# First channels loaded in quarters, first query products in four PSUM banks with their high terms first, bias row cast in one piece

## The reference

```python
q = x @ Wq.T + bq;  k = x @ Wk.T + bk;  v = x @ Wv.T + bv      # then split into 16 heads
q = softmax(q, axis=-1)          # over the 16 channels of a head
k = softmax(k, axis=-2)          # over the 1024 tokens
state = einsum('bhnd,bhne->bhde', k, v)
out = einsum('bhnd,bhde->bhne', q, state)        # heads joined again
out = layernorm(out) * ln_g + ln_b
x = layernorm(x + out @ Wo.T + bo)
h = layernorm(x) * ln1_g + ln1_b
h = layernorm(gelu(h @ ternary(w1).T + b1)) * ln2_g + ln2_b
x = layernorm(x + h @ ternary(w2).T + b2)
```

## Time and profile before

| | us |
|---|---|
| median of 3 runs (range) | 558.14 (557.33 to 558.61) |
| the profiled execution, its own time | 558.38 |
| its span in the profile | 556.4 |
| PE busy in the span | 533.2 (96%) |
| PEld, DVE, ACT, POOL busy | 490.5, 481.3, 481.7, 405.7 |
| first row of the queries' products on PE | 6.18 |
| first row of the keys' products of batch 0 | 13.66 |
| first row of `q_product(1, 0)` | 19.27 |

### The profile page before, as it was taken

The page is one execution under the profiler, slowest core; times in us unless marked ns, Lnnn a source line. Parts: engine busy times, 40 slices in busy tenths (PEclk is TensorE's granted clock), DMA queues, the critical chain, the costliest instruction groups (busy, mean ns, idle before and its releaser), DMA issues. The chain is left out here.

```text
span 556.4 us, 10878 instructions
## 1 busy us (share of the span) xinstructions
PE 533.2 (96%) x3533; PEld 490.5 (88%) x3533; DVE 481.3 (86%) x1230; ACT 481.7 (87%) x955; POOL 405.7 (73%) x420
## 2 busy tenths in 40 slices
PE   8999999999999999989899999999999999999991
PEld 7999999898999989779788998999999999999890
DVE  5878998989899898948687899999999999999895
ACT  5746798798979878778889999999999999999993
POOL 3965979877787977476558876876776776676693
PEclk9999999999999999999999999999999999999996
DMA  8530050411605030241111022222012222110012
GB/s 340 201 113 0 4 226 2 173 56 69 234 1 228 1 115 39 75 155 75 76 40 33 13 71 77 77 76 68 39 50 77 77 77 77 45 34 38 39 39 113
DMA packets 12679, 46.51 MB, mean 84 GB/s; under 512 B 1360, under 2 KB 3792, under 8 KB 10448
## 3 DMA queue, kind: packets, MB, share of 16 engines
q1 hardware_dynamic: 12336, 45.28, 22.6%
q10 hardware_dynamic: 288, 0.54, 0.3%
HBM read 29.01 MB, written 16.81 MB: 82 GB/s over the span
## 5 line engine op out<-in xcount | busy, mean ns | idle before, releaser
L1957 PE MATMUL qps_sps_aps_then_y<-ff_w_over_xc_lo,ff_a_lo_over_qw 128*128 128x258 f32 x512 | 126.7, 283 | 0.0
L1957 PE MATMUL qps_sps_aps_then_y<-ff_w_over_xc_lo,ff_a_hi_over_xc_lo 128*128 128x258 f32 x512 | 126.6, 283 | 0.0
L1308 DVE SCALAR_TENSOR_TENSOR ff_a_lo_over_qw<-ring,ff_rho,ff_a_hi_over_xc_lo 128x512 fp32r<-128x512 f32 x128 | 93.0, 745 | 15.5 <-ACT ff_a_hi_over_xc_lo L847 14.6
L1933 PE MATMUL ring<-ff_ht_hi_over_qw,t 128*128 128x512 f32 x256 | 104.0, 406 | 0.9 <-DVE ff_ht_lo_over_xc_hi L1300 0.5
L1933 PE MATMUL ring<-ff_ht_lo_over_xc_hi,t 128*128 128x512 f32 x256 | 100.7, 393 | 0.0
L1957 PEld LDWEIGHTS qps_sps_aps_then_y<-ff_w_over_xc_lo,ff_a_hi_over_xc_lo 128*128 128x128 f32 x512 | 96.9, 189 | 3.6
L1957 PEld LDWEIGHTS qps_sps_aps_then_y<-ff_w_over_xc_lo,ff_a_lo_over_qw 128*128 128x128 f32 x512 | 96.6, 189 | 3.4
L829 ACT ACTIVATE ring<-ring,bias 128x512 f32<-128x512 f32 x128 | 84.0, 685 | 7.8 <-PE ring L1933 6.8
L553 POOL TENSOR_TENSOR ff_accp_over_xt_lo<-ff_accp_over_xt_lo,ff_sq_over_ek_et_hi 128x512 f32<-128x512 f32 x66 | 86.1, 1304 | 2.9
L845 ACT ACTIVATE ff_sq_over_ek_et_hi<-ring 128x512 f32<-128x512 f32 x128 | 80.6, 630 | 0.5
L847 ACT CAST ff_a_hi_over_xc_lo<-ring 128x512 fp32r<-128x512 f32 x128 | 79.5, 621 | 0.0
(11 more groups left out here) (191 smaller groups left out, 1605.0 us busy)
## 6 DMA issues: line engine op xcount, KB each, us to landing
xt<-in_x_tok_dram SPq DMA_DIRECT2D x8, 1024.0 KB, 4.8
out_dram<-ff_z_over_et_lo SPq DMA_DIRECT2D x15, 512.0 KB, 3.2
x_scratch<-z SPq DMA_DIRECT2D x14, 514.0 KB, 3.1
ff_x_over_w_raw_xc<-x_scratch SPq DMA_DIRECT2D x14, 514.0 KB, 4.9
xc<-in_x_chan_dram SPq DMA_DIRECT2D x6, 1024.0 KB, 6.9
w_raw<-in_w_dram SPq DMA_DIRECT2D x2, 1024.0 KB, 6.0
ek<-in_x_chan_dram SPq DMA_DIRECT2D x1, 1024.0 KB, 8.1
x_scratch<-xt SPq DMA_DIRECT2D x2, 512.0 KB, 5.5
```

Of the source, the lines that this page charges most:

```text
L1308: nc.vector.scalar_tensor_tensor(out=ff_a_lo[:, m % DEPTH], in0=ff_bank(k, m), scalar=ff_rho[:, m:m + 1], in1=ff_a_hi[:, m % DEPTH].bitcas ...
L1933: mm = nc.tensor.matmul(ff_bank(k, m), t1[:, c, m * P:(m + 1) * P], h[:, k % 2, c], start=(c == 0 and j == 0), stop=(c == CH - 1 and j == 1))
L1957: last = nc.tensor.matmul(ff_yps[:, t, 0:C + 2], a[:, m % DEPTH, t * P:(t + 1) * P], ff_w2[:, m], start=(m == 0 and j == 0), stop=(m == FC ...
```

## The change

Five edits, all at the start of the program:

1. The host lays batch 0's channels out in quarters. ACT issues quarter 0 and quarter 1 as a transfer each; SP issues quarters 2 and 3 as one. Three semaphores instead of two.
2. The four products of batch 0 get a bank each (`aps[:, 1]`, `qps`, `aps[:, 0]`, `sps`), so they don't wait for `q_sub`. `folded_wo_rows`, which writes two of these banks, waits for `q_sub` of all four, and the ACT seeds of `q_product(1, 0)` and `(1, 1)` wait for the first and the second.
3. Within a product the order of terms is high by high (needs the casts alone), high by low of Wq, low by high, for both halves of the quarter and both channel blocks each; then the bias row. PE waits for what the next term needs and no more.
4. The bias row's high part is one ACT cast of 512 columns instead of two of 256, its low part one DVE subtraction instead of two. On DVE it stands after `first_low(0)` instead of after `first_low(1)`, and the maximum and centring of quarter 0 stand ahead of `first_low(2)`.
5. `SPARKS` is 9 instead of 11.

```diff
-    SPARKS = 11
+    SPARKS = 9
+    FIRST_TERMS = (0, 2, 1)
...
-        def q_bank(v):
+        def q_bank(b, v):
+            if b == 0:
+                return (aps[:, 1], qps, aps[:, 0], sps)[v]
             return aps[:, 1] if v % 2 == 0 else qps
...
-            sp.dma_start(xc_first[:, 1], x_first[1]).then_inc(first_in[1], 16)
+            sp.dma_start(xc_first[:, 2:4], x_first[:, 2:4]).then_inc(first_in[2], 16)
...
-                act.wait_ge(q_sub, PAIRS * b + v - 1)
+                act.wait_ge(q_sub, v + 1 if b == 1 else PAIRS * b + v - 1)
...
-            act.dma_start(xc_first[:, 0], x_first[0]).then_inc(first_in[0], 16)
+            for q in range(2):
+                act.dma_start(xc_first[:, q], x_first[:, q]).then_inc(first_in[q], 16)
...
-                    for h in range(2):
-                        nc.scalar.copy(bq_parts[:, h], rows[:, ROW["bq"]]).then_inc(bq_hi_ok, 1)
-                act.wait_ge(first_in[q // 2], 16)
+                    nc.scalar.copy(bq_parts[:], rows[:, ROW["bq"]].rearrange("p (o c) -> p o c", o=1).to_broadcast(
+                        [P, 2, C])).then_inc(bq_hi_ok, 2)
+                act.wait_ge(first_in[min(q, 2)], 16)
...
             first_low(0)
+            dve.wait_ge(bq_hi_ok, 2)
+            split_lo(bq_parts[P // 2:], rows[P // 2:, ROW["bq"]].rearrange("p (o c) -> p o c", o=1).to_broadcast(
+                [P // 2, 2, C]), bq_parts[P // 2:]).then_inc(bq_ready, 2)
             first_low(1)
-            dve.wait_ge(bq_hi_ok, 2)
-            for h in range(2):
-                split_lo(bq_parts[P // 2:, h], rows[P // 2:, ROW["bq"]], bq_parts[P // 2:, h]).then_inc(bq_ready, 1)
+            q_maximum(0, 0)
+            q_centre(0, 0)
             first_low(2)
-            for v in range(PAIRS):
+            for v in range(1, PAIRS):
...
-            pe.wait_ge(w_ready[0], 1)
+            pe.wait_ge(w_high[0], 1)
 
             def folded_wo_rows():
                 pe.wait_ge(w_scaled, 2 * CH)
+                pe.wait_ge(q_sub, PAIRS)
...
+            def first_q_product(v):
+                pe.wait_ge(first_hi_ok, v + 1)
+                for n, k in enumerate(FIRST_TERMS):
+                    if n == 1:
+                        pe.wait_ge(w_ready[0], 1)
+                    elif n == 2 and v < 3:
+                        pe.wait_ge(first_lo_ok, v + 1)
+                    elif n == 2:
+                        pe.wait_ge(second_lo_ok, 1)
+                    for h in range(2):
+                        for c in range(CH):
+                            a, w = q_operands(0, v, h, c)[k]
+                            nc.tensor.matmul(q_bank(0, v)[:, h * C:(h + 1) * C], a, w, start=(n + h + c == 0), stop=False,
+                                             skip_group_check=True)
+                pe.wait_ge(bq_ready, 2)
+                q_bias_row(0, v, False).then_inc(q_mm, 1)
```

More of the change, by code:

```diff
@@ L213, in both_halves @@
         bq_in, rows_in = sem("bq_in"), sem("rows_in")
-        first_in = [sem(f"first_in{h}") for h in range(2)]
+        first_in = [sem(f"first_in{h}") for h in range(3)]
         first_hi_ok, first_lo_ok, second_lo_ok = sem("first_hi_ok"), sem("first_lo_ok"), sem("second_lo_ok")
@@ L722, in q_bias @@
                     wait_for(act, y_out, T * (b - 2))
-                nc.scalar.copy(q_bank(v).rearrange("p (a c) -> p a c", c=C),
+                nc.scalar.copy(q_bank(b, v).rearrange("p (a c) -> p a c", c=C),
                                rows[:, ROW["bq"]].rearrange("p (o c) -> p o c", o=1).to_broadcast([P, 2, C])
@@ L1687, in ternary_rows, with q_bias_row, q_operands @@
                     mm.then_inc(f_rows, 1)
-            def q_bias_row(v, start):
-                return nc.tensor.matmul(q_bank(v), part[:], bq_parts[:].rearrange("p a c -> p (a c)"), start=start,
+            def q_bias_row(b, v, start):
+                return nc.tensor.matmul(q_bank(b, v), part[:], bq_parts[:].rearrange("p a c -> p (a c)"), start=start,
                                         stop=not start, skip_group_check=True)
+            def q_operands(b, v, h, c):
+                ts = slice((2 * v + h) * P, (2 * v + h + 1) * P)
+                return split3(xc_hi[b % 2][:, c, ts], xc_lo[b % 2][:, c, ts], w_hi[:, 0, c], w_lo[:, 0, c])
@@ L1693, in q_product @@
             def q_product(b, v):
-                if not 0 <= b < NB:
+                if not 1 <= b < NB:
                     return
-                if b == 0:
-                    if v < 3:
-                        pe.wait_ge(first_lo_ok, v + 1)
-                    else:
-                        pe.wait_ge(second_lo_ok, 1)
-                elif v == 0:
+                if v == 0:
                     pe.wait_ge(xc_lo_ok, CH * b)
                     wait_for(pe, y_out, T * (b - 2))
-                if b >= 1 and v in SEEDED:
+                if v in SEEDED:
@@ L1705, in q_product @@
                     pe.wait_ge(q_seed, len(SEEDED) * (b - 1) + v + 1)
                 else:
-                    wait_for(pe, q_sub, PAIRS * b + v - 1)
-                    if b >= 1:
-                        q_bias_row(v, True)
+                    pe.wait_ge(q_sub, PAIRS * b + v - 1)
+                    q_bias_row(b, v, True)
                 for h in range(2):
-                    ts = slice((2 * v + h) * P, (2 * v + h + 1) * P)
-                    out = q_bank(v)[:, h * C:(h + 1) * C]
                     for c in range(CH):
-                        for k, (a, w) in enumerate(split3(xc_hi[b % 2][:, c, ts], xc_lo[b % 2][:, c, ts],
-                                                          w_hi[:, 0, c], w_lo[:, 0, c])):
-                            last = nc.tensor.matmul(out, a, w, start=(b == 0 and h == 0 and c == 0 and k == 0),
-                                                    stop=(b >= 1 and c == CH - 1 and k == 2),
-                                                    skip_group_check=True)
@@ L1719, in q_product @@
-                if b == 0:
-                    if v == 0:
-                        pe.wait_ge(bq_ready, 2)
-                    last = q_bias_row(v, False)
+                        for k, (a, w) in enumerate(q_operands(b, v, h, c)):
+                            last = nc.tensor.matmul(q_bank(b, v)[:, h * C:(h + 1) * C], a, w, start=False,
+                                                    stop=(c == CH - 1 and k == 2), skip_group_check=True)
                 last.then_inc(q_mm, 1)
             for v in range(PAIRS):
-                q_product(0, v)
+                first_q_product(v)
```

11 lines of the change are left out of this document (5 added, 6 removed).

## The result

The changed kernel takes 559.5 us (median of 19 runs, 558.6 to 560.63), the kernel before 558.01 us (19 runs, 556.99 to 558.67). The ratio is 1.0028, with an interval of 1.0021 to 1.0035. The forecast was 556.6, so the sign was wrong. The profiled execution of after took 559.0 us with a span of 556.9. It lies half a us under its median, that of before 0.37 above.

The account below looks back on a forecast made before the run. PE, busy 533.2 of 556.4 us, was taken as the bound. It would be 1.76 us ahead at the keys, capped at 1.5 by the wait for POOL: 558.14 - 1.5 = 556.6 us, range 555.8 to 558.2.

Parts of the forecast that it names:

- For quarter 0 I count bytes: Start of the products: quarter 0 and Wq, 524 kB, moved by 3.45 us; ACT's cast runs from 4.05 to 4.65.
- the 4.7 to 5.0 for quarter 1: Ahead of the first bias row: quarter 1 lands at 4.7 to 5.0 us by the same byte count.
- Nothing in the change shortens that: the same bytes lie ahead of `ek`: Operands of `q_product(1, 0)`: `ek`'s cast stays at 10.67 us, POOL's low parts end at 17.62, capping the advance at 1.5.
- The rival for `ek`: Loading ahead of `ek`: smaller pieces delay it by up to 0.63 us; gain 0.9, time 557.2 us; chance 0.12.
- The stall at the bias row: PE at product 1's bias row: a wait of 0.1 to 0.4 us for `bq_ready`, taken as 0.3 with its slow start.
- the clock rose while the nine ran: PE's start: TensorE reaches 2.4 GHz during the nine sparks, so 256-column product matmuls cost 0.117 us each.
- The rival that made this decide the sign: Batch 0's products: a late clock adds 0.1 us per matmul; no gain from 15 on, at worst 562 us; chance 0.05.
- the advance at the keys: Start of the keys on PE: 11.9 instead of 13.66 us, so PE is 1.76 us ahead.
- no wait for `q_sub`: Third product of batch 0: the four banks remove PE's wait of 0.61 us plus its slow start.
- a shift of PE at this place is passed on: Behind `q_product(1, 0)`: the 1.5 us advance survives margins of 0.4 and 0.2 us, then everything later follows PE.
- The wait for POOL at 17.8: Ahead of `q_product(1, 0)`: PE would wait for POOL's low parts and start at 17.78 us, losing 0.2 to 0.3 us.
- `first_low(2)`, which I had end at 9.5: DVE's low part of quarter 2, behind a maximum and a centring: ends at 9.5 us, PE needs it at 9.6 or later.

Follow-up runs that it names:

- experiment 4: The kernel before with only the change's loading (three transfers, rows of 8 KB per partition); 559.62 us, ratio 1.0026 to the kernel before.
- experiment 8: The changed kernel with 512 B of padding per partition's row, so rows of 8.5 KB; 557.63 us, ratio 0.9986 to the kernel before.
- experiment 1: The changed kernel with quarter 0, quarter 1 and the second half each contiguous in HBM, same transfers; 557.54 us, ratio 0.9989 to the kernel before.
- experiment 5: The changed kernel with 14 sparks instead of 9; 559.44 us, ratio 1.002 to the kernel before.
- Experiment 9: The changed kernel with contiguous quarters, each bias row one product later, `first_low(2)` ahead of the first maximum; 557.3 us, ratio 0.9986 to the kernel before.
- experiment 6: The changed kernel with 14 sparks and ACT's cast of the bias row ahead of quarter 1; 559.14 us, ratio 1.001 to the kernel before.
- experiment 11: The changed kernel with HBM rows padded from 8 to 12 KB per partition; 556.54 us, ratio 0.9976 to the kernel before.
- experiment 12: The changed kernel with HBM rows padded from 8 to 32 KB per partition; 557.61 us, ratio 0.999 to the kernel before.
- experiment 2: The changed kernel with the loading of before (two contiguous halves), all other edits kept; 557.49 us, ratio 0.9987 to the kernel before.
- experiment 7: The changed kernel with quarters 0 and 1 side by side in rows of 4 KB, second half contiguous; 557.78 us, ratio 0.9991 to the kernel before.
- experiment 10: The changed kernel with HBM rows padded from 8 to 16 KB per partition; 558.48 us, ratio 1.0008 to the kernel before.

## Why the prediction was wrong

**The step that failed** is "For quarter 0 I count bytes". I took 418 GB/s from a window in which every transfer in flight read contiguous blocks, and applied it to reads of 2 KB out of 8 KB rows. So "moved by 3.45" and "a cast from 4.05" became a cast at 6.00, and the 4.7 to 5.0 for quarter 1 became 7.74. The sentence "Nothing in the change shortens that: the same bytes lie ahead of `ek`" has the same fault: the bytes are the same, their rate isn't, and `ek` came 1.66 us later. The layout stood in the change, in the host's array and in the index that moved from `x_first[0]` to `x_first[:, q]`. I priced the number of transfers and not what one of them reads. Experiments 4 (this loading alone gives the whole loss) and 8 (512 B of padding remove it) show it.

The count was wrong for contiguous blocks too, by less. It also took over the slices of before from 1 to 3 us, 43 and 293 GB/s. In experiment 1 these are 18 and 113, quarter 0 is cast at 4.71 instead of 4.05, and quarter 1 at 5.76 instead of 4.7 to 5.0. The first cost nothing, since the sparks ended later still; the second carried over to the bias row (below).

**The rival for `ek`** priced the delay as one more transfer, at most 0.63 us, and put it in the wrong place. In after POOL's chain of `ek` is late, but ends before PE asks for it. POOL of the changed kernel:

```profile
14.38 4.90 POOL L426 TENSOR_TENSOR xc_lo<-ek,xc_hi 128x1024 fp32r<-128x1024 f32 x2 [0.91 <-ACT xc_hi L673]
```

It ends at 19.28, and `q_product(1, 0)` starts at 20.58. The advance wasn't capped there; it had been lost at the first bias row.

**The stall at the bias row** was foreseen as 0.3 us, with the right chain and the right remark that every later matmul stands behind it. From the cast of quarter 1 to the bias row I had 1.9 us, and it took 1.99. Only the start was wrong, by 2.7 to 3.0 us; the keys came 3.07 us later than forecast.

**The clock.** "the clock rose while the nine ran" held in before, and not in after, where the matmuls are 0.21 us apart up to 9.5 us. The rival that made this decide the sign was still wrong: experiment 5 took the cost away and the keys stayed where they were.

**Why a good loading gives only half.** In experiment 1 the second product starts at 8.09, where the forecast implies 6.99, and the advance at the keys is 0.66 us instead of 1.76. The 1.1 us are those of the bias row's chain: quarter 1 is cast at 5.76, some 0.9 later than forecast, and the bias row follows 1.99 us behind, at 7.75. Sparks that end at 5.4 instead of 4.9 and four terms at 1.2 GHz, 0.8 us together, are hidden behind that chain, since PE still waits 0.31 us for it. Experiment 9 takes the chain away and brings the keys to 12.56. There the clock counts: the first product starts at 5.31 instead of 4.95, and its twelve terms take 2.1 us instead of 1.4, which is the 0.7 us that are missing to 11.9 (less the stall of 0.4 in the forecast).

**What held:** 1.64 us per product, no wait for `q_sub`, 5.61 us for the keys, and that a shift of PE at this place is passed on, here for 230 us, in the wrong direction. The store at 246 us, which hides 0.8 us of the delay in the profile of after, stands in no term of the prediction. The wait for POOL at 17.8 never came, since PE was never early enough: in experiment 9, the earliest, POOL ends at 17.01 and PE asks at 18.16. And `first_low(2)`, which I had end at 9.5, is harmless only while it doesn't meet POOL (below).

## What to carry to other kernels

When a change splits a transfer, look at the addresses that it reads before counting its bytes: compare the host's array and the index, and give each piece a block of its own, or pad the row; a rate read from contiguous transfers doesn't price strided ones. A DMA share near 1 with few GB/s in a window is the sign of it, and transfers that weren't touched are late with it. Where a byte count starts from the first microseconds of a profile, take these slices from more than one kernel: from 2 to 3 us they moved 113 to 293 GB/s here. When an early operand gates a wait that stands ahead of a long queue (here the bias row ahead of three products), move the wait behind work that is ready, and check for a second chain that arrives at the same moment before giving either the blame.

## What the runs showed of the hardware that I had not expected

**Reads 8 KB apart.** Pieces of 2 KB at a distance of 8 KB moved 116 to 180 GB/s from 3 to 5 us in four kernels (after, 4, 5, 6). At 4, 8.5, 12, 16 and 32 KB the same windows show 247 to 404. The dependence isn't monotonic: 16 KB is in between (quarter 1 cast at 6.13), and 12 and 32 KB delay quarter 0 but not quarter 1. Nor is the distance alone enough: in after the same rows are read with 349 and 360 GB/s from 5 to 7 us, and a packet of quarter 1 takes 0.10 us where one of quarter 0 took 0.21. What makes the first read of rows 8 KB apart slow is not shown. In experiments 11 and 12 Wq is cast at 4.90 and 4.93, late as in after (4.97); that isn't explained either.

**DVE and POOL exclude each other for subtractions out of SBUF.** A low part of 512 columns takes DVE 0.69 us. When it starts while POOL makes one of its own, it ends 0.54 to 0.56 us after POOL does, whenever it started (experiments 2, 6, 7, 8 and 10): 1.45 us in experiment 6 (rows above), and in experiment 2 1.23 us, where DVE's row starts at 9.38 and POOL's runs from 8.78 for 1.29. DVE:

```profile
9.38 1.23 DVE L1088 TENSOR_TENSOR xc_lo<-xc,xc_hi 128x512 fp32r<-128x512 f32 x1
```

POOL:

```profile
8.78 1.29 POOL L562 TENSOR_TENSOR xc_lo<-xc,xc_hi 128x512 fp32r<-128x512 f32 x1 [7.77 <-ACT xc_hi L878]
```

It holds the other way round: in after POOL's low part of Wk starts at 11.76, while DVE has been making one since 11.64, and takes 1.71 us instead of the 1.29 of the earlier trace rows. DVE's maximum and its centring read PSUM and show no such stretch beside POOL (0.68 and 0.69). The Trainium skill's page "SBUF — State Buffer", section Terms, describes a port pair that these two engines share under an exclusive lock, and the rows agree with it: the later one goes on only when the earlier one is done. The change moves `first_low(2)` two places down, into POOL's time: a cost of the edit that the prediction didn't name, 0.34 us of waiting on PE in experiment 6 and a gap of 0.24 us ahead of the same term in experiment 2. No run isolates it.

**The moment at which TensorE's clock rises.** PE starts on the sparks near 1.18 us in all kernels, and its matmuls go over to 2.4 GHz distances somewhere between the last sparks and 9.65 us, latest in after, where PE idled for 1.38 us in between. Nine sparks took 4.21 us in the changed kernel and most variants, and 3.85 in experiment 12; the first four product matmuls took 1.20 in after and 0.71 in experiment 5. Even without a gap it differs: experiments 8 and 10 give PE the same work up to there and start the first product at 5.26, but the second four terms take 1.05 us in one and 0.63 in the other. A chain that hangs on PE's first 10 us can move by some tenths of a us by this alone.
